# First stage of a token tower: denominators moved to ScalarE, VectorE's instructions in another order

## The chip, the cores and the metric

The kernel runs on one core of a Trainium2 chip. The metric is the device time of one execution in microseconds (us); smaller is better. The core's engines run side by side, each through its own list of instructions in order, and wait for one another by semaphores: TensorE (PE: products and transposes into PSUM banks), VectorE (DVE), ScalarE (ACT), GpSimd (POOL) and SyncE (SP, which issues transfers).

## The reference, cut to what matters

64 x 128 tokens go through an embedding, a layer with linear attention, and a layer with 16 experts. The change lies in the attention:

```python
pq, pk = (_phi(q), _phi(k))                      # phi(x) = elu(x) + 1
kv = jnp.einsum('bshd,bshm->bhmd', pk, v)
z = 1.0 / (jnp.einsum('bshd,bhd->bsh', pq, pk.sum(axis=1)) + 1e-06)
attn = jnp.einsum('bshd,bhmd,bsh->bshm', pq, kv, z)
...
h = tok(x)                                       # embedding of the tokens, 256 wide
h = h + attn(layernorm(h))                       # 16 heads of 16
h = h + ffn(layernorm(h))                        # gates, two of 16 experts, causal attention
```

`z` is one divided by the sum for each head plus 1e-6: the sums plus that constant are the denominators.

## The kernel before, in words

One tile is one sequence: 128 tokens on 128 partitions, 256 values each; there are 64 tiles (B). The kernel has three stages one after another: the first (embedding, attention, second norm, gate scores, places of the tokens with their experts; to about 360 us), the products of the experts' weights with the sorted tokens (to about 560 us), and the causal attention with the output products. The first stage also splits the experts' weights into a high part (ScalarE, L548) and a low part (VectorE, L553, `weight_lo`), one weight a step in 48 of the steps.

In the first stage every engine runs a function `step1(i)` for i from -7 on, written out, one call after another; nothing but the order of the calls and the semaphores orders the work. In one step the engines work on different tiles: the first norm of tile i+4, the attention's exponentials of tile i+3, its sums of tile i+2, the second norm of tile i+1, the gate scores of tile i. By the names used below:

- `centers` (VectorE, L1235) turns the roots that GpSimd formed (L768) into the shifts of both norms. It is the first thing of VectorE's step.
- x1 (ScalarE, L927) is the first norm of tile i+4; it waits for `centers`. TensorE turns it (L1662), ScalarE casts the turned tile (x1_T, L943, written to `split_hi`), VectorE forms the rest (x1_lo, L1310, written to `split_lo`).
- Behind x1_lo TensorE forms the q/k product (L1677 with the bias, then L1681) and the v product. In the next step ScalarE applies Relu (L917) and Exp (L921) to q and k, and VectorE adds them to phi (L1302).
- phi is turned, and key times value is summed (L1757); VectorE masks it by heads: the big kvm product (L1321) and the small one (L1323). In the next step TensorE forms the sums of numerators and denominators from both (L1709).
- VectorE then forms `den` (L1240: the sums plus 1e-6), the reciprocal (L1243, `zden`), `attn` (L1245) and the residual h2 (L1254), which SyncE stores.
- bn_stats and the aggregate of h2 (L1258, L1260), with the first norm's aggregate (L1314) and statistics (L1079), lead by `roots_in` (L1266, L1267) to GpSimd's roots and so to the `centers` of the next step.
- Every fourth tile closes a group of four for the gates. Its pieces are spread over four steps near the end of VectorE's step: `experts_chosen`, `experts_numbered`, `rows_counted` (L1205 writes `before_rows`), `rows_placed`. TensorE's part, the rank product (L1691, L1692), waits for `before_rows` and stands at the beginning of TensorE's step, ahead of the sums (L1709).

ScalarE's step is, in order: Relu, Exp, x1, x2 (the second norm, L888), the copy of v (L935), x1_T, two more copies (L948, L894), the cast of a weight (L548). VectorE's is: `centers`, `weight_lo`, phi, `den`, reciprocal, `attn`, x1_lo, first aggregate, h2, big kvm, small kvm, bn_stats of h2, its aggregate, `roots_in`, the gates' piece, statistics of the next rows. The tail of the stage (last tiles) runs interleaved with the beginning of the second stage.

Of the kernel before, what the change touches and what calls it, by code (L numbers as in the profile page):

```python
# [44 lines left out]
P = 128  # L45
# [56 lines left out]
def build(nc, x_turned, embed, W_qkv, b_qkv, W_proj, b_proj, sim_matrix, gates, q_proj, k_proj, v_proj, o_proj, out):  # L102
# [37 lines left out]
    with ExitStack() as ctx:  # L140
# [19 lines left out]
        causal_r = sb("causal_r", [P, P], F32R)  # L160
        zeros = sb("zeros", [P, C])
        minus_half = sb("minus_half", [P, E])
        eps = sb("eps", [P, 3])
        expert_no = sb("expert_no", [P, E])
        region_start = sb("region_start", [P, E])
        tile_no = sb("tile_no", [P, 1])
# [184 lines left out]
        o_scaled = sem("o_scaled")  # L351
        o_pooled = sem("o_pooled")
        o_added = sem("o_added")
        N_CONSTS = 16

        EARLY_GROUP = EARLY_TOKENS // QUAD - 1
        N_EARLY_OPS, N_EARLY_TAB = 17, 9
# [337 lines left out]
        def _(pool):  # L695
# [26 lines left out]
            pool.memset(used[:, E:E + 1], 0.0).then_inc(consts_ready, 1)  # L722
            pool.memset(eps[:, 0:2], LN_EPS).then_inc(consts_ready, 1)
            pool.memset(eps[:, 2:3], NORM_EPS).then_inc(consts_ready, 1)
            pool.memset(before_rows[:, :, :].bitcast(F32), 0.0).then_inc(consts_ready, 1)
            pool.iota(expert_no[:, :], pattern=[[1, E]], base=0, channel_multiplier=0,
                      allow_small_or_imprecise_dtypes=True).then_inc(consts_ready, 1)
# [143 lines left out]
        def _(act):  # L871
# [24 lines left out]
            def split_and_copy(i):  # L896
# [6 lines left out]
                if i.inside(PAIR_TILES) and i.p:  # L903
# [5 lines left out]
                    pair, m = y_slot(i)  # L909
                    act.copy(pair[:, m, :], ps_y[i.c % len(ps_y)][:, 0:Y]).then_inc(done["pair_copied"], 1)  # L910

            def step1(i):
                tile = i.shift(3)
                if tile.inside(B):

                    after(act, "qk_product", tile)
                    act.activation(qk_neg[:, :], ps_qk[:, :], ACT.Relu, scale=-1.0  # L917
                                   ).then_inc(done["qk_negative"], 1)
                    after(act, "qk_negative", tile)
                    after(act, "phi", tile.shift(-1))  # L920
                    act.activation(qk_e[:, :], qk_neg[:, :], ACT.Exp, scale=-1.0).then_inc(done["qk_exp"], 1)  # L921
                tile = i.shift(4)
                if tile.inside(B):
                    t = tile.c
                    after(act, "x1_turned", tile.shift(-1))
                    after(act, "centers", tile)
                    act.activation(x1[:, :], h[t % 8], ACT.Identity, scale=roots[:, t, 0:1],  # L927
                                   bias=centers[:, t, 0:1]).then_inc(done["x1_normed"], 1)
                if i.shift(1).inside(B):
                    second_norm(i.shift(1))  # L930
                tile = i.shift(3)
                if tile.inside(B):
                    after(act, "v_product", tile)
                    after(act, "kv_product", tile.shift(-1))
                    act.copy(vx[:, :, 0:P], ps_v[:, 0:C].rearrange("p (g n) -> p g n", g=G)  # L935
                             ).then_inc(done["v_copied"], 1)
                if i.c == TAIL_STEP - 1:
                    split_and_copy(Tile(-2))
                tile = i.shift(4)
                if tile.inside(B):  # L940
                    after(act, "x1_turned", tile)
                    after(act, "v_product", tile.shift(-1))
                    act.copy(x1T_s[0], ps_x1[:, 0:C]).then_inc(done["x1_T"], 1)  # L943
                tile = i.shift(3)
                if tile.inside(B):
                    after(act, "phi_q_turned", tile)
                    after(act, "attn_sums", tile.shift(-1))
                    act.copy(pqT[:, :, :].rearrange("p g t -> p (g t)"), ps_pq[:, 0:C]  # L948
                             ).then_inc(done["phi_q_T"], 1)
                if i.shift(1).inside(B):  # L950
                    second_turned(i.shift(1))
                for n in weights_at(i.c):
                    weight_hi(act, n)
# [3 lines left out]

            def tail(k):

                if k == 5:  # L960
                    second_norm(Tile(B - 2))
                if k == 8:
# [88 lines left out]
        def _(dve):  # L1051
# [183 lines left out]
                dve.scalar_tensor_tensor(centers[:, row, :], moments[:, row, :, 0], -1.0, roots[:, row, 0:2],  # L1235
                                         ALU.mult, ALU.mult).then_inc(done["centers"], 1)

            def attention_formed(tile):
                after(dve, "attn_sums", tile)
                dve.tensor_scalar(den[:, :, :], ps_sums[:, :, P:NUMW], DEN_EPS, None, ALU.add  # L1240
                                  ).then_inc(done["attn_den"], 1)
                after(dve, "attn_den", tile)
                dve.reciprocal(zden[:, :, :], den[:, :, :]).then_inc(done["attn_z"], 1)  # L1243
                after(dve, "attn_z", tile)
                dve.tensor_tensor(attn[:, :].rearrange("p (g h d) -> p g h d", g=G, d=D),  # L1245
                                  ps_sums[:, :, 0:P].rearrange("p g (h d) -> p g h d", d=D),
# [9 lines left out]
            def second_stats(tile):  # L1256
                after(dve, "h2", tile)
                dve.bn_stats(stats[:, 2 * tile.p + 1, :], h2[tile.p][:, :]).then_inc(done["ln2_stats"], 1)  # L1258
                after(dve, "ln2_stats", tile)
                dve.bn_aggr(moments[:, tile.c + 3, 1, :], stats[:, 2 * tile.p + 1, :]  # L1260
                            ).then_inc(done["ln2_moments"], 1)
# [22 lines left out]
            def step1(i):  # L1284
# [8 lines left out]
                    gates_formed()  # L1293
                if i.c == 0:
                    gate_columns_scaled()
                for n in weights_at(i.c - 1):
                    weight_lo(dve, n)
                if phi_tile.inside(B):

                    after(dve, "kv_product", phi_tile.shift(-1))  # L1300
# [1 line left out]
                    dve.scalar_tensor_tensor(phi[:, :], ps_qk[:, :], 0.0, qk_e[:, :], ALU.max, ALU.add  # L1302
                                             ).then_inc(done["phi"], 1)
                if attn_tile.inside(B):
                    attention_formed(attn_tile)
                if i.c == TAIL_STEP - 1:
                    split_and_copy(Tile(-2))
                if x1_tile.inside(B):
                    after(dve, "x1_T", x1_tile)
                    dve.tensor_tensor(x1T_s[1], ps_x1[:, 0:C], x1T_s[0].bitcast(F32), ALU.subtract  # L1310
                                      ).then_inc(done["x1_lo"], 1)
                if ln1_tile.inside(B):
                    after(dve, "ln1_stats", ln1_tile)
                    dve.bn_aggr(moments[:, ln1_tile.c, 0, :], stats[:, 2 * i.p, :]).then_inc(done["ln1_moments"], 1)  # L1314
                if attn_tile.inside(B):
                    residual_added(attn_tile)
                if phi_tile.inside(B):

                    after(dve, "attn_sums", phi_tile.shift(-1))
                    after(dve, "kv_product", phi_tile)  # L1320
                    dve.tensor_tensor(kvm[:, :, 0:P], ps_kv[:, :, 0:P],  # L1321
                                      head_mask[:, :].unsqueeze(1).broadcast_to([P, G, P]), ALU.mult)
                    dve.tensor_tensor(kvm[:, :, P:NUMW], ps_kv[:, :, P:P + 1].broadcast_to([P, G, HG]),  # L1323
                                      head_of_row[:, :].unsqueeze(1).broadcast_to([P, G, HG]), ALU.mult
                                      ).then_inc(done["kv_masked"], 1)
# [1 line left out]
                    split_and_copy(Tile(-1))  # L1327
                if attn_tile.inside(B):
                    second_stats(attn_tile)
                row = i.c + 5  # L1330
                if 0 <= row < N_ROOTS:
                    root_inputs(row, attn_tile)
# [71 lines left out]
            def tail(k):  # L1404
# [3 lines left out]
                if k == 2:  # L1408
                    experts_numbered(last_group - 2)
                if k == 3:  # L1410
                    attention_formed(Tile(B - 1))
                    residual_added(Tile(B - 1))
                    second_stats(Tile(B - 1))
                    root_inputs(N_ROOTS - 1, Tile(B - 1))
                if k == 4:
                    centers_formed(N_ROOTS - 2)
# [524 lines left out]
```

## Time and profile before

| | |
|---|---|
| time, median of 3 runs | 995.45 us (992.7 to 995.6) |
| profiled execution: time, span | 992.72 us, 990.9 us |
| TensorE busy over the span | 925.8 us (93%) |
| VectorE busy | 838.2 us (85%) |
| ScalarE busy | 600.0 us (61%) |
| GpSimd busy | 668.9 us (68%) |
| mean granted clock of TensorE | 0.987 of full speed |

The span is the profiled time from the first instruction to the last. Busy shares are means over stages of different kinds, so they are read by stretch. Consecutive instructions of VectorE and ScalarE may overlap a little in the trace: the next can start before the one in front has ended.

### The profile page before, as it was taken

How to read it: one execution, taken by the hardware profiler on the slowest of the kernel's cores; microseconds unless marked ns; L12 is line 12 of the kernel's file. 1: busy time of each engine (PE TensorE's matmuls, PEld its weight loads, DVE VectorE, ACT ScalarE, POOL GpSimd, SP SyncE). 2: the span in 40 equal slices, each digit the busy share in tenths (PEclk: the TensorE clock that was granted, in tenths of full speed). 3: DMA queues.
4: the chain of work that ended last, by engine and by line, in shares of the span. 5: the costliest groups of instructions: out<-in, count | busy, mean ns of one | idle time of the engine just before them, and what ended most of it. 6: DMA issues, size and time to landing. Idle time of an engine off the chain costs nothing.

```text
span 990.9 us, 20545 instructions
## 1 busy us (share of the span) xinstructions
PE 925.8 (93%) x5231; PEld 798.1 (81%) x5231; DVE 838.2 (85%) x2910; ACT 600.0 (61%) x1633; POOL 668.9 (68%) x881
## 2 busy tenths in 40 slices
PE   4999999999899989989999599999999999999998
PEld 4777788887777889979899578888888888888876
DVE  3789999999999987556665369999999999999998
ACT  4566676676667554435444266666666766666664
POOL 5447777777777655795000268888888888888885
PEclk9999999999999999989999889999999999999999
DMA  2113444444343349878898423333333333333231
GB/s 66 49 60 123 127 130 155 144 149 130 113 128 115 99 159 333 281 251 274 279 294 266 156 84 104 107 107 107 107 98 103 100 100 107 107 107 103 90 102 38
DMA packets 104762, 137.54 MB, mean 139 GB/s; under 512 B 13762, under 2 KB 91586, under 8 KB 104644
## 3 DMA queue, kind: packets, MB, share of 16 engines
q1 hardware_dynamic: 86196, 82.93, 26.6%
q0 software_dynamic: 18176, 52.45, 17.4%
q8 instruction: 49, 0.80, 0.3%
q10 hardware_dynamic: 272, 0.79, 0.2%
q14 instruction: 69, 0.57, 0.2%
HBM read 70.06 MB, written 66.06 MB: 137 GB/s over the span
## 4 chain that ended last, share of the span: by engine, by line
PE 60%; DVE 26%; issue 6%; POOL 3%; DMA 2%; ACT 2%; SPq 1%; POOLq 0%; DVEq 0%; ACTq 0%
PE bank L1655 16%; PE bank L1656 16%; PE bank L1657 16%; PE bank L1662 6%; DVE phi L1302 4%; DVE attn L1245 2%; DVE kvm L1321 2%; DVE stats L1258 2%; PE bank L1681 2%; DVE stats L1079 2%; DVE zden L1243 1%; PE bank L1899 1%; PE bank L1905 1%; POOL sorted_x L786 1%; DVE moments L1260 1%
## 5 line engine op out<-in xcount | busy, mean ns | idle before, releaser
L1655 PE MATMUL bank<-wo_hi,split_lo 128*128 128x512 f32 x512 | 214.6, 419 | 1.5 <-DVE split_lo L1623 0.8
L1656 PE MATMUL bank<-wo_lo,split_hi 128*128 128x512 f32 x512 | 203.3, 397 | 0.0
L1657 PE MATMUL bank<-wo_hi,split_hi 128*128 128x512 f32 x512 | 203.3, 397 | 0.0
L860 POOL DMA_INDIRECT row_y<-sorted_y,pair_now x128 | 130.7, 1021 | 31.2 <-issue 22.3
L1009 ACT ACTIVATE h<-bank,rwo 128x256 f32<-128x256 f32 x256 | 106.8, 471 | 26.5 <-PE bank L1657 13.9
L1657 PEld LDWEIGHTS bank<-wo_hi,split_hi 128*128 128x128 f32 x512 | 96.8, 189 | 23.1
L1655 PEld LDWEIGHTS bank<-wo_hi,split_lo 128*128 128x128 f32 x512 | 96.9, 189 | 21.5 <-DVE x L1592 1.6
L1592 DVE SCALAR_TENSOR_TENSOR x<-bank,rwo,x 128x256 f32<-128x256 f32 x256 | 111.1, 475 | 1.2 <-PE bank L1657 1.2
L1656 PEld LDWEIGHTS bank<-wo_lo,split_hi 128*128 128x128 f32 x512 | 97.5, 190 | 17.5
L1592 DVE SCALAR_TENSOR_TENSOR qk_e<-bank,rwo,qk_e 128x256 f32<-128x256 f32 x256 | 110.9, 474 | 0.2 <-PE bank L1657 0.2
L1655 PE MATMUL bank<-wq_hi,split_lo 128*128 x288 | 110.6, 384 | 0.0
L768 POOL TENSOR_TENSOR roots<-roots_in,minus_half 128x3 f32<-128x3 f32 x67 | 59.9, 894 | 74.4 <-DVE roots_in L1267 74.4
L917 ACT ACTIVATE qk_neg<-bank 128x512 f32<-128x512 f32 x64 | 38.3, 598 | 113.2 <-PE bank L1681 113.2
L778 POOL DMA_INDIRECT sorted_x<-row_y,position_u x80 | 80.9, 1011 | 31.1 <-issue 23.1
L1275 DVE TENSOR_TENSOR split_lo<-bank,split_hi 128x256 fp32r<-128x256 f32 x144 | 60.6, 421 | 46.1 <-ACT split_hi L901 45.0
L1656 PE MATMUL bank<-wq_lo,split_hi 128*128 x288 | 98.1, 341 | 0.0
L1657 PE MATMUL bank<-wq_hi,split_hi 128*128 x288 | 97.8, 340 | 0.0
L1009 ACT ACTIVATE phi<-bank,rwo 128x256 f32<-128x256 f32 x128 | 53.7, 471 | 68.9 <-PE bank L1657 68.9
L1681 PE MATMUL bank<-wo_hi,split_lo 128*128 128x512 f32 (+1 forms) x256 | 87.4, 342 | 0.0
L1681 PE MATMUL bank<-wo_lo,split_hi 128*128 128x512 f32 (+1 forms) x256 | 87.2, 340 | 0.0
L1681 PE MATMUL bank<-wo_hi,split_hi 128*128 128x512 f32 (+1 forms) x256 | 87.1, 340 | 0.0
L901 ACT CAST split_hi<-bank 128x256 fp32r<-128x256 f32 x144 | 53.8, 375 | 46.7 <-PE bank L1662 45.1
(242 smaller groups left out, 2529.4 us busy)
## 6 DMA issues: line engine op xcount, KB each, us to landing
sorted_y<-w_attn SPq DMA_DIRECT2D x40, 384.0 KB, 3.4
sorted_y<-row_y SPq DMA_DIRECT2D x24, 384.0 KB, 3.6
h_rows<-h SPq DMA_DIRECT2D x64, 128.0 KB, 1.7
row_x<-h_rows SPq DMA_DIRECT2D x64, 128.0 KB, 3.5
out_h<-row_x SPq DMA_DIRECT2D x64, 128.0 KB, 2.1
h<-sorted_x SPq DMA_DIRECT2D x48, 128.0 KB, 3.3
phi<-sorted_x SPq DMA_DIRECT2D x24, 128.0 KB, 3.5
qk_neg<-sorted_x SPq DMA_DIRECT2D x24, 128.0 KB
```

The costliest lines, as they stand in the source:

```text
L768: pool.tensor_tensor(roots[:, row, :], roots_in[:, row, :], minus_half[:, 0:3], ALU.pow).then_inc(done["roots"], 1)
L778: pool.indirect_dma_start(out=sorted_x, out_offset=offsets(position_u[:, t, n:n + 1]), in_=x2[t % N_X2], in_offset=None).then_inc(scattere ...
L860: pool.indirect_dma_start(out=row_y[:, 2 * tile.p + n, :], out_offset=None, in_=sorted_y, in_offset=offsets(pair_now[tile.q][:, n:n + 1])) ...
L901: act.copy(split[tile.q][0][:, :, :].rearrange("p c t -> p (c t)"), ps_turn[tile.p][:, 0:C]).then_inc(done["pair_hi"], 1)
L1009: act.mul(part[:, j, :], ps[:, j * C:(j + 1) * C], rwo[tile.p][:, e:e + 1]).then_inc(o_scaled, 1)
L1275: dve.tensor_tensor(lo, ps_turn[tile.p][:, 0:C], hi.bitcast(F32), ALU.subtract).then_inc(done["pair_lo"], 1)
L1592: dve.scalar_tensor_tensor(acc[j][:, :], src, weight, base[:, :], ALU.mult, ALU.add).then_inc(o_added, 1)
L1655: pe.matmul(ps, left[1][c], right[0][c], start=(c == 0), stop=False)
L1656: pe.matmul(ps, left[0][c], right[1][c], start=False, stop=False)
L1657: last = pe.matmul(ps, left[0][c], right[0][c], start=False, stop=(c == n - 1))
L1662: last = pe.transpose(ps[:, n * P:(n + 1) * P], piece, ident[:, :])
L1681: last = pe.matmul(ps[:, 0:hi - lo], turned[x][c], w_attn_s[w][:, c, lo:hi], start=False, stop=end)
```

## The change

The denominators move from VectorE to ScalarE: an Identity activation with the constant 1e-6 as a bias per row, between Exp and x1, waiting for the sums. A fourth column of `eps` holds the constant, so GpSimd sets one more constant. On VectorE `attention_formed` is split into the reciprocals and the rest, `second_stats` into statistics and moments, and the order of the step changes: `weight_lo` goes from behind `centers` to between the statistics and the moments of h2; `attn` goes behind x1_lo; h2 goes between the two kvm products. In the tail the last tile's denominators stand on ScalarE at the same place (k = 3).

```diff
@@ constants
-        eps = sb("eps", [P, 3])
+        eps = sb("eps", [P, 4])
-        N_CONSTS = 16
+        N_CONSTS = 17
+            pool.memset(eps[:, 3:4], DEN_EPS).then_inc(consts_ready, 1)
@@ ScalarE
+            def denominators(tile):
+                after(act, "attn_sums", tile)
+                after(act, "attn_z", tile.shift(-1))
+                act.activation(den[:, :, :], ps_sums[:, :, P:NUMW], ACT.Identity, bias=eps[:, 3:4]
+                               ).then_inc(done["attn_den"], 1)
...
                     act.activation(qk_e[:, :], qk_neg[:, :], ACT.Exp, scale=-1.0).then_inc(done["qk_exp"], 1)
+                if i.shift(2).inside(B):
+                    denominators(i.shift(2))
...
+                if k == 3:
+                    denominators(Tile(B - 1))
@@ VectorE
-            def attention_formed(tile):
-                after(dve, "attn_sums", tile)
-                dve.tensor_scalar(den[:, :, :], ps_sums[:, :, P:NUMW], DEN_EPS, None, ALU.add
-                                  ).then_inc(done["attn_den"], 1)
+            def attention_inverses(tile):
                 after(dve, "attn_den", tile)
                 dve.reciprocal(zden[:, :, :], den[:, :, :]).then_inc(done["attn_z"], 1)
+
+            def attention_formed(tile):
                 after(dve, "attn_z", tile)
...
-                for n in weights_at(i.c - 1):
-                    weight_lo(dve, n)
...
                 if attn_tile.inside(B):
-                    attention_formed(attn_tile)
+                    attention_inverses(attn_tile)
...
                     dve.tensor_tensor(x1T_s[1], ps_x1[:, 0:C], x1T_s[0].bitcast(F32), ALU.subtract
                                       ).then_inc(done["x1_lo"], 1)
+                if attn_tile.inside(B):
+                    attention_formed(attn_tile)
                 if ln1_tile.inside(B):
...
-                if attn_tile.inside(B):
-                    residual_added(attn_tile)
                 if phi_tile.inside(B):
...
                     dve.tensor_tensor(kvm[:, :, 0:P], ps_kv[:, :, 0:P],
                                       head_mask[:, :].unsqueeze(1).broadcast_to([P, G, P]), ALU.mult)
+                if attn_tile.inside(B):
+                    residual_added(attn_tile)
+                if phi_tile.inside(B):
                     dve.tensor_tensor(kvm[:, :, P:NUMW], ps_kv[:, :, P:P + 1].broadcast_to([P, G, HG]),
...
                 if attn_tile.inside(B):
                     second_stats(attn_tile)
+                for n in weights_at(i.c - 1):
+                    weight_lo(dve, n)
+                if attn_tile.inside(B):
+                    second_moments(attn_tile)
...
                 if k == 3:
+                    attention_inverses(Tile(B - 1))
                     attention_formed(Tile(B - 1))
                     residual_added(Tile(B - 1))
                     second_stats(Tile(B - 1))
+                    second_moments(Tile(B - 1))
```

## Rows read from the trace of the kernel before

**Rows 1.** Stretches: length, busy us (instructions) by engine, granted clock, DMA share, GB/s.
```profile
core 0: us, PE busy (x) PEld busy (x) DVE busy (x) ACT busy (x) POOL busy (x), PEclk, DMA share, GB/s
0.00:20.00 20.00, 7.97 (x28) 6.37 (x29) 7.44 (x22) 8.03 (x16) 12.76 (x37) 1.00 0.24 75
60.00:350.00 290.00, 266.98 (x1749) 231.03 (x1748) 271.04 (x1275) 194.59 (x479) 205.27 (x209) 1.00 0.40 125
420.00:430.00 10.00, 5.28 (x23) 4.87 (x22) 2.60 (x6) 1.90 (x5) 9.33 (x17) 0.76 0.63 198
```
**Rows 2.** Instructions in order of time (start, length in us), ScalarE, 48 steps apart.
```profile
71.16 0.58 ACT L927 ACTIVATE x<-h,centers,roots 128x256 f32<-128x256 f32 x1
...
329.45 0.63 ACT L921 ACTIVATE qk_e<-qk_neg 128x512 f32<-128x512 f32 x1
329.99 0.58 ACT L927 ACTIVATE x<-h,centers,roots 128x256 f32<-128x256 f32 x1
```
**Rows 3.** In order of time, one step of ScalarE: Relu, Exp, x1, x1_T, next Relu.
```profile
187.91 0.60 ACT L917 ACTIVATE qk_neg<-bank 128x512 f32<-128x512 f32 x1 [1.65 <-PE bank L1681]
188.54 0.63 ACT L921 ACTIVATE qk_e<-qk_neg 128x512 f32<-128x512 f32 x1
189.13 0.60 ACT L927 ACTIVATE x<-h,centers,roots 128x256 f32<-128x256 f32 x1
...
190.38 0.37 ACT L943 CAST split_hi<-bank 128x256 fp32r<-128x256 f32 x1
...
193.25 0.60 ACT L917 ACTIVATE qk_neg<-bank 128x512 f32<-128x512 f32 x1 [1.65 <-PE bank L1681]
```
**Rows 4.** In order of time, the same step of VectorE, to the next centers.
```profile
188.89 0.14 DVE L1235 SCALAR_TENSOR_TENSOR centers<-moments,roots 128x2 f32<-128x2 f32 x1
188.95 0.41 DVE L553 TENSOR_TENSOR wq_lo<-raw,wq_hi 128x256 fp32r<-128x256 f32 x1
189.28 0.68 DVE L1302 SCALAR_TENSOR_TENSOR phi<-bank,qk_e 128x512 f32<-128x512 f32 x1
189.89 0.16 DVE L1240 TENSOR_SCALAR den<-bank 128x16 f32<-128x16 f32 x1
190.08 0.25 DVE L1243 RECIPROCAL zden<-den 128x16 f32<-128x16 f32 x1
190.37 0.42 DVE L1245 TENSOR_TENSOR attn<-bank,zden 128x256 f32<-128x256 f32 x1
190.78 0.42 DVE L1310 TENSOR_TENSOR split_lo<-bank,split_hi 128x256 fp32r<-128x256 f32 x1
191.12 0.17 DVE L1314 BATCH_NORM_AGGREGATE moments<-stats 128x2 f32<-128x6 f32 x1
...
191.93 0.42 DVE L1258 BATCH_NORM_STATS2 stats<-h 128x6 f32<-128x256 f32 x1
192.38 0.18 DVE L1260 BATCH_NORM_AGGREGATE moments<-stats 128x2 f32<-128x6 f32 x1
192.67 0.17 DVE L1266 TENSOR_SCALAR roots_in<-moments 128x2 f32<-128x2 f32 x1
...
193.15 0.80 DVE L1205 TENSOR_TENSOR before_rows<-before_rows,top_two 128x16 fp32r<-128x16 f32 x4
...
194.20 0.14 DVE L1235 SCALAR_TENSOR_TENSOR centers<-moments,roots 128x2 f32<-128x2 f32 x1
```
**Rows 5.** In order of time, TensorE: sums, q/k product, rank product, the next sums.
```profile
188.53 0.63 PE L1709 MATMUL bank<-kvm,pqT 128*128 128x136 f32 x4
...
191.35 0.47 PE L1677 MATMUL bank<-bias,ones_r 128*128 128x512 f32 x1
...
194.00 0.30 PE L1691 MATMUL bank<-top_two,earlier_r 128*128 128x64 f32 x1
...
194.24 0.71 PE L1709 MATMUL bank<-kvm,pqT 128*128 128x136 f32 x4
```
**Rows 6.** By line, ScalarE's 16-column operations: duration ns min/median/max, first and last start.
```profile
L874 ACT ACTIVATE gate_bias<-gate_tmp x1: 216/216/216, 5.6 to 5.6; 128x16 f32<-128x16 f32 x1
...
L1042 ACT ACTIVATE rwo<-routing,psumm x64: 307/310/323, 574.6 to 978.8; 128x16 f32<-128x16 f32 x64
```

More of the change, by code:

```diff
@@ L1258, in second_stats, with second_moments @@
                 dve.bn_stats(stats[:, 2 * tile.p + 1, :], h2[tile.p][:, :]).then_inc(done["ln2_stats"], 1)
+            def second_moments(tile):
                 after(dve, "ln2_stats", tile)
```

## The prediction, made before the result was known

> **What bounds the kernel now.** I read the stretches first: from 60 to 350 us, the body of the first stage, TensorE is busy for 267.0 of 290 us and VectorE for 271.0, both over 92% [rows 1]. Shares that close do not say which engine sets the step, so I followed one step of each engine in order of time. The step repeats: from the x1 of one step (71.16) to the x1 48 steps on (329.99) is 258.83 us, 5.39 us a step [rows 2].
>
> Two closed loops run through a step. I count from start to start.
>
> *The ScalarE loop.* x1 (189.13) is followed by its turn on TensorE and by the cast of the turned tile, x1_T (190.38): 1.25. VectorE's x1_lo begins 0.40 later (190.78), which is the cast's 0.37 and 0.03 more: x1_lo starts when the cast lets it, and not before [rows 3, 4]. Behind x1_lo TensorE starts the q/k product (191.35), and ScalarE's Relu of it starts at 193.25, 2.47 after x1_lo; the Exp 0.63 after the Relu; the next x1, where nothing else holds it, 0.54 after the Exp (329.45 to 329.99) [rows 2 to 5]. Sum: 1.25 + 0.40 + 2.47 + 0.63 + 0.54 = 5.29.
>
> *The VectorE loop.* x1 also needs `centers`, which VectorE forms first in its step: centers at 188.89, x1 at 189.13, 0.24 [rows 3, 4]. So from centers to x1_lo there are 0.24 + 1.25 + 0.40 = 1.89 us that VectorE's order can't shorten. From x1_lo round to the next centers (190.78 to 194.20) are 3.42. Sum: 5.31.
>
> The kernel sits where both loops are nearly equal. What VectorE does inside the 1.89 us is free as long as it fits: weight_lo, phi, den, reciprocal and attn stand there now (188.95 to 190.78) and just fill it [rows 4]. What it does after x1_lo is paid in full.
>
> **The change part by part.**
>
> *Order of VectorE.* The new order is centers, phi, reciprocal, x1_lo, attn, first aggregate, the big kvm product, h2, the small kvm product, bn_stats of h2, weight_lo, its aggregate, and the rest as before. Two instructions move from the free side of x1_lo to the paid side: attn (190.37, 0.42 long) and weight_lo (188.95, 0.41). Neighbours that don't read each other start 0.08 before the end of the one in front (weight_lo takes 0.33 from start to start, x1_lo's successor starts 0.34 after it), so they add 0.34 + 0.34. Given back: bn_stats to its aggregate takes 0.45 now, since the aggregate reads it (0.42 + 0.03); with weight_lo between them bn_stats takes 0.34, so -0.11. Lost again: bn_stats of h2 now comes two behind h2 and starts when h2 is written, about +0.03, the size of the wait in front of the reciprocal (189.89 + 0.16 to 190.08). In all 0.34 + 0.34 - 0.11 + 0.03 = +0.60 from x1_lo to centers [rows 4]. The ends: 0.68 if nothing is given back; 0.41 if the pause behind that aggregate (192.38, 0.18 long, the next at 192.67, 0.19 more than in a close pair) goes as well.
>
> The 0.11 between a dependent and an independent pair is this trace's [rows 4]. The Trainium skill, page "VectorE: DVE Perf Modes", section "The DRAIN you can't avoid", says that a wait between chained operations costs nothing beyond the flush that every operation pays; the trace disagrees by that 0.11. By the page the addition would be 0.34 + 0.34 = 0.68, and the 48 steps with a weight would lose 3.8 us more.
>
> The denominator's 0.16 and its wait in front of the reciprocal, and the wait from reciprocal to attn, lie in the 1.89 and give nothing back: VectorE is ready for x1_lo some 0.06 + 0.61 + 0.28 = 0.95 us after centers and then stands still for about 0.9 us, until the cast comes. Without that cover they would be worth 0.19 + 0.11.
>
> New VectorE loop: 3.42 + 0.60 + 1.89 = 5.91 for this step; over the 36 of the 48 steps that have no rank product I take +0.59 (0.01 of a step was slack of centers).
>
> *Denominators on ScalarE.* The instruction stands between Exp and x1, so x1, x2, the v copy and the casts queue behind its wait for the sums. The sums end at 189.16 (188.53 + 0.63), 1.25 after the Relu and just at the end of the Exp (189.17) [rows 3, 5]. The trace of before has no such operation; the nearest are ScalarE's 16-column operations, 0.216 without a scale per row and 0.310 with one [rows 6]. Less 0.10 of overlap with x1 (the Exp is 0.63 long, x1 starts 0.54 behind it) they delay x1 by 0.12 to 0.21. I take 0.15, nearer the first, and 0.05 for the semaphore (0.03 to 0.10). An operation that is hidden whole would be 0.
>
> The Trainium skill, page "ScalarE: Activation LUTs", section "What ACT_TABLE_LOAD costs", prices an ACTIVATE with a bias per row at 280 ns + 0.833 ns a column, with 93 ns overlapped: an estimate of 0.20 for 16 columns, which would add 0.05 to the steps that this loop bounds, 1.2 us in all.
>
> ScalarE loop in a plain step: 2.47 + 1.25 + 0.05 + 0.15 + 1.25 + 0.40 = 5.57. That is under VectorE's 5.9 while weights are split, so there the ScalarE part costs nothing by itself. In the 11 steps up to 76 us no weight is split; there VectorE's addition is only 0.26 (no weight_lo) and ScalarE's loop decides: 5.57 against about 5.28, ten times +0.29, and +1.0 once where a rank product falls: 3.9 us. The last three steps: about 0.7.
>
> *Where both meet: the rank steps.* In every fourth step TensorE makes a rank product ahead of the sums. It waits for VectorE's `before_rows` (193.15 + 0.80 = 193.95; rank at 194.00), and the sums end at 194.95, 4.17 behind x1_lo [rows 4, 5]. Nothing was late by that: VectorE came to the sums only behind phi. Now ScalarE waits for them in front of x1, and before_rows itself comes 0.60 later. So x1_lo to sums 4.77, semaphore 0.05, denominators 0.15, then 1.65 to x1_lo: 6.62 instead of 5.31, +1.31. There are 12 such steps in the 48: 15.7 us.
>
> *The rest.* h2 comes about 0.7 us later behind x1_lo, and with it SyncE's store of h2 and, behind that in its queue, the next weight's load; the weight's cast is the last thing of ScalarE's step, so I cost this at nothing; a weight that came late would add its lateness to weight_lo. The one memset more in the set-up and the denominators in the tail I also take as nothing (under 0.5 us together).
>
> *Sum.* 36 x 0.59 = 21.2; rank steps 15.7; steps without weights 3.9; last steps 0.7: 41.5 us. Later stages start later and keep their length. The profiled execution took 992.72 us (span 990.9); 992.72 + 41.5 = 1034.2. That is 2.7 below the median of the runs shown, 995.45, and at their lowest, 992.7; the median of the new runs may lie either way, and I put the forecast at 1035.
>
> **The rivals.**
> 1. *VectorE is relieved, as its 93% suggests.* Without den and the dependent pairs VectorE has 0.4 us less to issue. If the order did not hold x1_lo to the cast, the step would sink to the ScalarE loop of 5.29, at most 0.10 x 48 = 5 us: 990. Against it: x1_lo starts 0.03 behind the cast already, so an earlier place can't make it earlier [rows 3, 4]. The Trainium skill, page "Perfetto Trace Analysis", section "Optimizing Scalar/DVE Operations", advises moving work to ScalarE when VectorE is saturated; by that rule this rival wins. Chance 0.04.
> 2. *Only ScalarE's loop pays.* If the instructions behind x1_lo found room, because centers stopped deciding x1, then plain steps cost 5.57 - 5.39 = 0.18 (6.5 us), rank steps 2.47 + 1.70 + 0.05 + 0.15 + 1.65 = 6.02, +0.71 (8.5 us), others 4: 19 us, 1012. Against it: in the step shown centers alone explains x1. Chance 0.12.
> 3. *It cancels out*, within 0.3%: both additions lie in waits that I read wrongly. Chance 0.04.
> 4. *The clock falls.* TensorE's share in the stage sinks from 92% to about 81% (times 5.39 / 6.15). In the ten microseconds from 420 TensorE was idle for 4.7 and the granted clock was 0.76; over the first 20 us, 40% busy, it was 1.00 [rows 1]. If a tenth of the clock went, some 3.5 us of TensorE work in each of 60 steps would cost 21 us more: 1055. Chance 0.06.
>
> **How the numbers follow.** The forecast has 0.74. Its own range: with an addition of 0.41 in place of 0.60 the 48 steps lose 0.19 x 48 = 9.1 us less, 1025; with 0.68 they lose 3.8 more, and the upper prices on ScalarE (0.06 + 0.05 in 24 steps) 2.6 more, 1041. To hold 8 in 10 the range reaches down to rival 2: 1011 to 1042. Chances: slower by over 0.3% (about what a measurement of this kernel tells from no change) 0.74 + 0.12 + 0.06 = 0.92, the same 0.04, faster 0.04.
>
> **What would show it.** Right: in the new trace x1_lo still starts 0.03 behind the cast, but with some 0.9 us of VectorE idle before it, released by ScalarE (over 40 us in the stage); x1_lo to centers near 4.0; steps of 5.9 to 6.1, rank steps near 6.6; VectorE's share in the stage near 80%; denominators on ScalarE of 0.2 to 0.3 us that start right behind the sums; the loss complete by the end of the first stage. Wrong: x1_lo without idle time before it (rival 1), rank steps like the others (rival 2), a granted clock under 1.00 (rival 4), or later stages that give time back.

## The result, and the profile after

The changed kernel takes 1037.43 us (median of 4 runs, 1036.1 to 1038.38); the kernel before, run beside it, 995.32. The ratio is 1.0428, 95% interval 1.0407 to 1.0449: slower by 4.3%. The profiled execution took 1038.38 us with a span of 1036.5, against 992.72 and 990.9 before, so the two traces differ by 45.6 us of span. The medians leave out two far slower runs, one of weight_only (1801.41) and one of the kernel before (1275.7).

The stretch from 60 to 350 us, in the columns of [rows 1], and the longest waits between 60 and 335 us (engine, line, what it waited for: us in all, times, longest us) for VectorE and ScalarE:

```profile
60.00:350.00 290.00, 239.43 (x1531) 207.42 (x1530) 223.93 (x1070) 184.50 (x468) 177.74 (x184) 0.98 0.36 112
...
DVE split_lo L1320 <- ACT split_hi L952: 46.1, 44, 1.3
DVE zden L1251 <- ACT den L916: 3.9, 11, 0.6
...
ACT den L916 <- PE bank L1728: 12.3, 12, 1.3
ACT x L936 <- DVE centers L1246: 6.9, 20, 0.6
```

VectorE has fallen from 271.0 busy us [rows 1] to 223.9, TensorE from 267.0 to 239.4: no engine is short of room, and yet the step is longer. `split_lo` is x1_lo. It now has VectorE idle in front of it in 44 steps, 46.1 us in all between 60 and 335 us, and ScalarE's cast ends that wait. ScalarE in turn stands 12 times in front of `den`, which waits for TensorE's sums.

One rank step and the plain step behind it, all engines in order of time (the columns of [rows 2]). They answer to [rows 3 to 5]:

```profile
186.95 0.42 DVE L1320 TENSOR_TENSOR split_lo<-bank,split_hi 128x256 fp32r<-128x256 f32 x1 [0.98 <-ACT split_hi L952]
187.29 0.41 DVE L1255 TENSOR_TENSOR attn<-bank,zden 128x256 f32<-128x256 f32 x1
...
188.47 0.43 DVE L1268 BATCH_NORM_STATS2 stats<-h 128x6 f32<-128x256 f32 x1
188.81 0.41 DVE L553 TENSOR_TENSOR wq_lo<-raw,wq_hi 128x256 fp32r<-128x256 f32 x1
189.13 0.17 DVE L1272 BATCH_NORM_AGGREGATE moments<-stats 128x2 f32<-128x6 f32 x1
...
189.89 0.80 DVE L1216 TENSOR_TENSOR before_rows<-before_rows,top_two 128x16 fp32r<-128x16 f32 x4
190.05 0.63 ACT L928 ACTIVATE qk_e<-qk_neg 128x512 f32<-128x512 f32 x1
190.75 0.30 PE L1710 MATMUL bank<-top_two,earlier_r 128*128 128x64 f32 x1 [0.54 <-DVE before_rows L1216]
190.95 0.14 DVE L1246 SCALAR_TENSOR_TENSOR centers<-moments,roots 128x2 f32<-128x2 f32 x1
190.99 0.71 PE L1728 MATMUL bank<-kvm,pqT 128*128 128x136 f32 x4
191.74 0.27 ACT L916 ACTIVATE den<-bank,eps 128x16 f32<-128x16 f32 x1 [1.06 <-PE bank L1728]
191.91 0.59 ACT L936 ACTIVATE x<-row_x,centers,roots 128x256 f32<-128x256 f32 x1
193.15 0.38 ACT L952 CAST split_hi<-bank 128x256 fp32r<-128x256 f32 x1
193.56 0.42 DVE L1320 TENSOR_TENSOR split_lo<-bank,split_hi 128x256 fp32r<-128x256 f32 x1 [1.26 <-ACT split_hi L952]
...
196.66 0.63 ACT L928 ACTIVATE qk_e<-qk_neg 128x512 f32<-128x512 f32 x1
197.32 0.27 ACT L916 ACTIVATE den<-bank,eps 128x16 f32<-128x16 f32 x1
197.48 0.14 DVE L1246 SCALAR_TENSOR_TENSOR centers<-moments,roots 128x2 f32<-128x2 f32 x1
197.72 0.60 ACT L936 ACTIVATE x<-row_x,centers,roots 128x256 f32<-128x256 f32 x1
198.97 0.37 ACT L952 CAST split_hi<-bank 128x256 fp32r<-128x256 f32 x1
199.37 0.42 DVE L1320 TENSOR_TENSOR split_lo<-bank,split_hi 128x256 fp32r<-128x256 f32 x1 [0.99 <-ACT split_hi L952]
```

*The rank step* runs from x1_lo at 186.95 to x1_lo at 193.56, 6.61 us. Follow what ended last: before_rows ends at 190.69, the rank product starts at 190.75, the sums behind it end at 191.70; the denominators start at 191.74, x1 at 191.91, and the cast lets x1_lo go 1.65 after x1. centers had been there since 191.09: it no longer decides.

*The plain step* runs from 193.56 to 199.37, 5.81 us. Here the denominators start at 197.32 and would let x1 go 0.17 later, at 197.49; it waits for centers and starts at 197.72, 0.24 after centers' start. centers itself comes 3.92 after x1_lo, since attn (187.29 in the step above) and weight_lo (188.81) now stand between them.

Step lengths from x1_lo to x1_lo over the whole stage, means in us, with their count; the very first step (6.87 before, 6.62 after) is left out:

| | first 11, no weight | 36 plain | 12 rank | last 3 | last x1_lo of the stage |
|---|---|---|---|---|---|
| before | 5.35 | 5.40 | 5.38 | 5.75 | 354.38 |
| after | 5.71 | 6.04 | 6.66 | 6.09 | 397.76 |
| all of it | +4.0 | +23.3 | +15.3 | +1.0 | +43.4 |

The stage ends 43.4 us later, of 45.6 in the span. The last 2 us come before the third stage: from the last x1_lo to the first of ScalarE's `rwo` operations ([rows 6], L1042) it is 220.3 us before and 222.7 after, and from there to the end of the span 416 in both.

### The profile page after: what moved, and what is told of

Same layout as the page of the kernel before. It is cut to its first block, busy times and chain, and to the rows that moved or that the text cites. A ratio compares the mean times of both kernels' runs of the same rounds, so it can differ in the third digit from the quotient of the medians.

```text
span 1036.5 us, 20609 instructions
## 1 busy us (share of the span) xinstructions
PE 930.8 (90%) x5231; PEld 802.6 (77%) x5231; DVE 817.4 (79%) x2846; ACT 618.7 (60%) x1697; POOL 663.7 (64%) x882
## 4 chain that ended last, share of the span: by engine, by line
PE 55%; DVE 19%; issue 8%; ACT 7%; POOL 7%; DMA 3%; SPq 1%; ACTq 0%; POOLq 0%; DVEq 0%
PE bank L1674 14%; PE bank L1675 14%; PE bank L1676 14%; PE bank L1681 5%; PE bank L1700 3%; DVE split_lo L1320 2%; DVE h L1264 2%; ACT split_hi L952 2%; DVE stats L1268 2%; ACT row_y L889 2%; POOL row_y L861 2%; DVE wq_lo L553 1%; POOL sorted_x L787 1%; PE bank L1728 1%; ACT x L889 1%
## 5 line engine op out<-in xcount | busy, mean ns | idle before, releaser
L861 POOL DMA_INDIRECT row_y<-sorted_y,pair_now x128 | 133.3, 1042 | 31.2 <-issue 22.3
L779 POOL DMA_INDIRECT sorted_x<-row_y,position_u x80 | 78.7, 983 | 31.6 <-issue 23.1
L1681 PE MATMUL bank<-ident,x 128*128 128x128 f32 x200 | 41.3, 289 | 54.9 <-ACT x L936 54.9
```

What stands on the lines that cost most here:

```text
L779: pool.indirect_dma_start(out=sorted_x, out_offset=offsets(position_u[:, t, n:n + 1]), in_=x2[t % N_X2], in_offset=None).then_inc(scattere ...
L861: pool.indirect_dma_start(out=row_y[:, 2 * tile.p + n, :], out_offset=None, in_=sorted_y, in_offset=offsets(pair_now[tile.q][:, n:n + 1])) ...
L1681: last = pe.transpose(ps[:, n * P:(n + 1) * P], piece, ident[:, :])
```

## The experiments

The theory is that of the prediction: two loops. In VectorE's, a step is the way from x1_lo to centers plus 1.89 us. In ScalarE's, when it carries the denominators, a step is x1_lo to Relu (2.47), Relu to the end of the sums, 0.04 and 0.17 to x1, 1.65 to x1_lo. The longer one is the step. The rival is that only one of the two is real: that the loss comes whole from ScalarE's new wait, or whole from VectorE's order. A further question was whether the two loops are what held the kernel before, or only what holds the one after. den_only, order_only, weight_only and attn_back ran beside the kernel before at 993.9 us, the kernels below them in the table beside it at 993.29; the changed kernel has its own comparison above.

All kernels, with the two measured quantities from which the loops are computed:

| | us | ratio (95%) | plain: x1_lo to centers | plain step | rank: Relu to end of sums | rank step |
|---|---|---|---|---|---|---|
| before | 993.9, 993.29 | | 3.50 | 5.40 | 1.77 | 5.38 |
| after | 1037.43 | 1.0428 (1.0407 to 1.0449) | 4.11 | 6.04 | 2.33 | 6.66 |
| den_only | 1011.82 | 1.0172 (1.0148 to 1.0196) | 3.50 | 5.59 | 1.74 | 6.07 |
| order_only | 1026.26 | 1.0319 (1.0300 to 1.0338) | 4.07 | 5.97 | 2.34 | 5.96 |
| weight_only | 1002.92 | 1.0078 (1.0052 to 1.0103) | 3.70 | 5.59 | 1.97 | 5.58 |
| attn_back | 1027.41 | 1.0332 (1.0314 to 1.0349) | 3.95 | 5.84 | 2.17 | 6.50 |
| attn_and_h2_back | 1016.31 | 1.0233 (1.0211 to 1.0255) | 3.72 | 5.66 | 1.95 | 6.28 |
| high_first | 991.45 | 0.9979 (0.9969 to 0.9989) | 3.50 | 5.39 | 2.11 | 5.39 |
| spread_pairs | 989.0 | 0.9959 (0.9944 to 0.9974) | 3.35 | 5.32 | 1.63 | 5.31 |
| both_loops | 981.52 | 0.9878 (0.9857 to 0.9899) | 3.35 | 5.24 | 1.96 | 5.24 |

The plain means of the changed kernel hold three steps in which TensorE's clock fell, those of order_only and attn_back one each (last section).

### Denominators alone (den_only)

The kernel before, with the denominators on ScalarE behind Exp and VectorE's order kept.

```diff
+            def denominators(tile):
+                after(act, "attn_sums", tile)
+                after(act, "attn_z", tile.shift(-1))
+                act.activation(den[:, :, :], ps_sums[:, :, P:NUMW], ACT.Identity, bias=eps[:, 3:4]
...
+                if i.shift(2).inside(B):
+                    denominators(i.shift(2))
...
-                dve.tensor_scalar(den[:, :, :], ps_sums[:, :, P:NUMW], DEN_EPS, None, ALU.add
-                                  ).then_inc(done["attn_den"], 1)
```

> The kernel before with the denominators on ScalarE and VectorE's order untouched but for the removed instruction. Theory of two loops: VectorE's paid side does not change, ScalarE's loop becomes 2.47 + 1.25 + 0.04 + 0.17 + 1.65 = 5.58 in plain steps (5.40 before) and 2.47 + 1.70 + 0.04 + 0.17 + 1.65 = 6.03 in rank steps (5.38 before), 5.58 in most early ones: +7 and +8 and +4 us, some 1014 us. Rival, that the new order alone loses and ScalarE has room for the denominators (it is busy 61%): 995 within 0.3%. Rival, that VectorE's work sets the stage: 0.19 less in 62 steps, 984.

It measured 1011.82, 17.9 us above the kernel before. The plain step is ScalarE's loop: 2.47 + 1.25 + 0.04 + 0.17 + 1.65 = 5.58 (measured 5.59); the rank step 2.47 + 1.74 + 0.04 + 0.17 + 1.65 = 6.07 (measured 6.07). A rank step on ScalarE, in order of time:

```profile
135.53 0.63 ACT L928 ACTIVATE qk_e<-qk_neg 128x512 f32<-128x512 f32 x1
136.65 0.28 ACT L916 ACTIVATE den<-bank,eps 128x16 f32<-128x16 f32 x1 [0.49 <-PE bank L1717]
136.82 0.59 ACT L936 ACTIVATE x<-row_x,centers,roots 128x256 f32<-128x256 f32 x1
```

The operation itself is the small part, 0.17 from its start to x1's. The larger one is that x1 now cannot start before the sums end: 0.49 us of waiting in this step, where x1 used to follow Exp by 0.54.

### The order alone (order_only)

The changed kernel with the denominators put back on VectorE, ahead of the reciprocals; all of the new order stays.

```diff
-            def denominators(tile):
-                after(act, "attn_sums", tile)
...
             def attention_inverses(tile):
+                after(dve, "attn_sums", tile)
+                dve.tensor_scalar(den[:, :, :], ps_sums[:, :, P:NUMW], DEN_EPS, None, ALU.add
+                                  ).then_inc(done["attn_den"], 1)
                 after(dve, "attn_den", tile)
```

> The new order of VectorE with the denominators left on VectorE, directly ahead of the reciprocal. Theory of two loops: from x1_lo to centers 0.60 more, so plain steps 5.99 instead of 5.40, rank steps no longer coupled through ScalarE and near 5.97 instead of 6.66; early steps nearly as before: +21 +7 +2 us, some 1026 us, and about 0.9 us of VectorE standing still in front of x1_lo less the denominator's 0.19. Rival, that ScalarE's instruction is the loss: 995 or a little under, since dependent pairs are spread.

It measured 1026.26. Both rank and plain steps are 5.96 to 5.97, VectorE's loop: 4.07 + 1.89 = 5.96. In the rank steps the sums end as late as in the changed kernel, 2.34 against 2.33 after the Relu, and it does not matter. One of them, in order of time, and the wait of x1 between 60 and 335 us:

```profile
137.71 0.63 ACT L921 ACTIVATE qk_e<-qk_neg 128x512 f32<-128x512 f32 x1
138.40 0.30 PE L1702 MATMUL bank<-top_two,earlier_r 128*128 128x64 f32 x1 [0.54 <-DVE before_rows L1205]
138.65 0.71 PE L1720 MATMUL bank<-kvm,pqT 128*128 128x136 f32 x4
138.84 0.60 ACT L927 ACTIVATE x<-row_x,centers,roots 128x256 f32<-128x256 f32 x1 [0.50 <-DVE centers L1235]
...
ACT x L927 <- DVE centers L1235: 24.7, 45, 0.9
```

x1 starts at 138.84, half a microsecond before these sums end (139.36); it waits for centers, 45 times, 24.7 us. So the late sums cost a rank step 0.70 (6.66 against 5.96) only through the denominators in ScalarE's queue. In the plain steps the denominators add nothing on top of the order: without the steps of lower clock the means are 5.97 and 5.96.

The parts do not add up: 17.9 us for the denominators alone and 32.4 for the order alone would be 50.3, and the change costs 42.1 in its own comparison. In plain steps the longer loop hides the other one: +0.19 for the denominators alone, +0.56 for the order alone, +0.57 for both (without the steps of lower clock).

### One of the two moved instructions (weight_only)

The kernel before, with weight_lo moved from behind centers to between the statistics and the moments of h2.

```diff
-                for n in weights_at(i.c - 1):
-                    weight_lo(dve, n)
...
                 if attn_tile.inside(B):
                     second_stats(attn_tile)
+                for n in weights_at(i.c - 1):
+                    weight_lo(dve, n)
+                if attn_tile.inside(B):
+                    second_moments(attn_tile)
```

> The kernel before with weight_lo alone moved to between the statistics and the moments of h2. Theory of two loops: paid side + 0.34 - 0.11 = + 0.23 in the 48 steps with a weight, a third of a microsecond of VectorE standing still in front of x1_lo: +11 us, 1006 us. Rival, that taking the wait out between the statistics and the moments helps: 0.11 less in 48 steps, 990.

It measured 1002.92. x1_lo to centers grew by 0.20 (3.50 to 3.70), and the 48 plain and rank steps by 0.19 and 0.20, 9.2 us, against 9.0 between the medians (5 to 10 by the interval of the ratio). An instruction of 0.41 us, moved from the covered side of x1_lo to the other, costs half of its length here: the part that it takes from the wait between the statistics and their aggregate comes back.

### attn put back (attn_back), and h2 with it (attn_and_h2_back)

The changed kernel with attn back in front of x1_lo:

```diff
                 if attn_tile.inside(B):
                     attention_inverses(attn_tile)
+                    attention_formed(attn_tile)
...
-                if attn_tile.inside(B):
-                    attention_formed(attn_tile)
```

> The changed kernel with attn put back ahead of x1_lo; everything else of the change stays. Theory of two loops: of the 0.60 on VectorE's paid side 0.34 go, so plain steps are set by both loops near 5.67, rank steps near 6.33 (the rows counted come 0.34 earlier): 25 us over the kernel before, 1020 us. Rival, that the place of attn does not matter: 1037.

A miss: 1027.41, 7 us above what was expected. x1_lo to centers is 3.95. With attn gone from behind x1_lo, the big kvm product stands directly behind the first aggregate and is ready before its input. In order of time:

```profile
334.46 0.63 PE L1775 MATMUL bank<-vx,phi 128*128 128x130 f32 x4
334.63 0.42 DVE L1321 TENSOR_TENSOR split_lo<-bank,split_hi 128x256 fp32r<-128x256 f32 x1 [0.80 <-ACT split_hi L952]
334.97 0.17 DVE L1325 BATCH_NORM_AGGREGATE moments<-stats 128x2 f32<-128x6 f32 x1
335.20 0.42 DVE L1330 TENSOR_TENSOR kvm<-bank,head_mask 128x256 f32<-128x256 f32 x1
```

The aggregate ends at 335.14 and a next operation that does not depend on it would start at 335.06, as the one behind x1_lo does 0.08 before its end; kvm starts at 335.20, 0.11 behind the end of TensorE's kv product (335.09). If that is the cause, h2 in front of kvm, where the kernel before has it, should cover the wait. The second kernel puts it back as well:

```diff
+                if attn_tile.inside(B):
+                    residual_added(attn_tile)
                 if phi_tile.inside(B):
...
-                if attn_tile.inside(B):
-                    residual_added(attn_tile)
-                if phi_tile.inside(B):
```

> The run attn_back with h2 put back ahead of the big kvm product as well. In attn_back that product stood 0.43 behind x1_lo and waited some 0.14 for TensorE's key-value product. Theory: that wait is what was missing from the 0.34, so plain steps 5.68 and rank steps 6.35, 7 us under attn_back: 1020 us. Rival, that attn's 0.34 is only half paid whatever stands behind it: 1027 as before.

It measured 1016.31, 4 us under what was expected, and x1_lo to centers is 3.72, that of weight_only (3.70), as it should be when weight_lo is the only thing left. The same place, in order of time:

```profile
337.19 0.63 PE L1774 MATMUL bank<-vx,phi 128*128 128x130 f32 x4
337.36 0.42 DVE L1321 TENSOR_TENSOR split_lo<-bank,split_hi 128x256 fp32r<-128x256 f32 x1 [0.53 <-ACT split_hi L952]
337.70 0.17 DVE L1325 BATCH_NORM_AGGREGATE moments<-stats 128x2 f32<-128x6 f32 x1
337.79 0.39 DVE L1264 TENSOR_TENSOR h<-row_x,attn 128x256 f32<-128x256 f32 x1
338.10 0.42 DVE L1332 TENSOR_TENSOR kvm<-bank,head_mask 128x256 f32<-128x256 f32 x1
```

h2 runs from 337.79 while the kv product ends (337.82), and kvm follows at its usual distance. h2's place cost 0.23 us a step in attn_back, more than the expectation put on it. The wait in the lines shown is 0.14 of it; another 0.07 lies in the distances between h2, the two kvm products and the statistics, which differ in the two orders. In the changed kernel attn stood in the gap instead of h2, so there the same wait was covered: in its step above the kv product ends at 187.42, and kvm starts at 187.71, 0.09 behind the aggregate's start.

The rank steps of both kernels fit ScalarE's loop with the sums' own lateness: 4.33 + 2.17 = 6.50 and 4.33 + 1.95 = 6.28, as measured (4.33 is 2.47 + 0.04 + 0.17 + 1.65).

### Shortening each loop of the kernel before (high_first, spread_pairs, both_loops)

If the kernel before sits where two loops are nearly equal, then shortening one should give little, and both more than the sum. high_first shortens ScalarE's: TensorE runs the products that don't read x1_lo before it waits for x1_lo.

```diff
+                after(pe, "x1_T", tile)
...
-                    for x, w, end in ((1, 0, False), (0, 1, False), (0, 0, c == CH - 1)):
-                        last = pe.matmul(ps[:, 0:hi - lo], turned[x][c], w_attn_s[w][:, c, lo:hi], start=False,
-                                         stop=end)
+                    for w in (1, 0):
+                        pe.matmul(ps[:, 0:hi - lo], turned[0][c], w_attn_s[w][:, c, lo:hi], start=False, stop=False)
+                after(pe, "x1_lo", tile)
+                for c in range(CH):
+                    last = pe.matmul(ps[:, 0:hi - lo], turned[1][c], w_attn_s[0][:, c, lo:hi], start=False,
+                                     stop=(c == CH - 1))
```

> The kernel before with only TensorE's order changed: bias and high products of q, k and v go ahead of the wait for x1_lo, the low products last. Theory of two loops: x1_lo leaves ScalarE's loop, which becomes shorter by TensorE's pause of 0.2 in front of the product (5.08), but VectorE's loop stays and sets nearly every step: 1 to 2 us less, not to be told from no change. Rival, that TensorE (92% busy) sets the stage: 0.2 in 60 steps, 12 us less.

spread_pairs shortens VectorE's: the first aggregate goes between the denominators and the reciprocals, in front of x1_lo, and the small kvm product between the statistics and the moments of h2.

```diff
                     denominators(attn_tile)
+                if ln1_tile.inside(B):
+                    after(dve, "ln1_stats", ln1_tile)
+                    dve.bn_aggr(moments[:, ln1_tile.c, 0, :], stats[:, 2 * i.p, :]).then_inc(done["ln1_moments"], 1)
...
                     second_stats(attn_tile)
+                if phi_tile.inside(B):
+                    dve.tensor_tensor(kvm[:, :, P:NUMW], ps_kv[:, :, P:P + 1].broadcast_to([P, G, HG]),
...
+                if attn_tile.inside(B):
+                    second_moments(attn_tile)
```

> The kernel before with two small instructions of VectorE moved into its dependent pairs and nothing carried from one side of x1_lo to the other in the wrong direction: the first aggregate goes between den and reciprocal, the small kvm product between the statistics and the moments of h2. Denominators stay on VectorE. Theory of two loops: paid side 0.09 + 0.08 = 0.17 shorter, but plain steps sink only to ScalarE's loop of 5.28: 5 us less, 989. Rival, VectorE alone: 0.17 + in 60 steps, 10 us less.

both_loops has both edits.

> high_first and spread_pairs together. Theory of two loops: ScalarE's loop 5.08, VectorE's 0.17 shorter: 11 us less, 983; more than the sum of the two alone (about 6.5). Rival, effects add: 6 to 7 us less.

Measured: 991.45 (-1.8 us), 989.0 (-4.3), and together 981.52 (-11.8), nearly twice the sum of 6.1. Each fits. In high_first the way from x1_lo to Relu falls from 2.47 to 2.14, and what x1 waits for changes; its waits between 60 and 335 us:

```profile
ACT qk_neg L917 <- PE bank L1685: 68.0, 51, 1.6
ACT x L927 <- DVE centers L1235: 17.0, 51, 0.7
```

x1 waits for centers in 51 steps, 17.0 us, and the plain step stays at VectorE's 3.50 + 1.89 = 5.39. Only the first 11 steps, where no weight is split, become shorter (5.35 to 5.22). The rival's 12 us, TensorE setting the stage, are not there. In spread_pairs VectorE's loop falls to 3.35 + 1.89 = 5.24, but the step to 5.32 only: ScalarE's loop, 5.29 in the prediction, now holds it, and x1 starts within 0.03 of 0.54 behind the Exp in 34 of the 48 steps (25 in the kernel before). In both_loops the step is 5.24, VectorE's loop to the hundredth. The stretch from 60 to 350 us of both_loops:

```profile
60.00:350.00 290.00, 262.35 (x1802) 234.48 (x1801) 274.17 (x1314) 201.96 (x489) 211.25 (x215) 1.00 0.41 129
```

VectorE's 274.2 busy us are only 3.1 more than before [rows 1], with 1314 instructions in the stretch against 1275.

The 0.15 us that spread_pairs takes out of VectorE's way (3.50 to 3.35) has two parts. The first aggregate now stands ahead of x1_lo, between the denominators and the reciprocals, and the small kvm product between the statistics and the moments of h2. In order of time:

```profile
337.66 0.16 DVE L1240 TENSOR_SCALAR den<-bank 128x16 f32<-128x16 f32 x1
337.74 0.17 DVE L1312 BATCH_NORM_AGGREGATE moments<-stats 128x2 f32<-128x6 f32 x1
337.86 0.25 DVE L1245 RECIPROCAL zden<-den 128x16 f32<-128x16 f32 x1
...
339.50 0.42 DVE L1260 BATCH_NORM_STATS2 stats<-h 128x6 f32<-128x256 f32 x1
339.83 0.16 DVE L1334 TENSOR_TENSOR kvm<-bank,head_of_row 128x16 f32<-128x16 f32 x1
339.95 0.18 DVE L1264 BATCH_NORM_AGGREGATE moments<-stats 128x2 f32<-128x6 f32 x1
```

The aggregate starts 0.08 before the denominators end. The reciprocals start 0.20 after the start of the denominators, where they started 0.19 after it with nothing in between [rows 4]: an instruction of 0.17 us goes into the chain for 0.01. From the statistics to their aggregate it takes 0.45 with the small product in between, as it did without it [rows 4]. Two things are mixed here, though: the small product is gained by the pair alone, while the aggregate also goes from the paid side of x1_lo to the covered one. No run separates them.

The Trainium skill, page "VectorE: DVE Perf Modes", section "The DRAIN you can't avoid", reports of eight copies that a semaphore after each "costs nothing extra here"; the same section says that "A next op that is not held starts earlier". In this trace an instruction that waits for the one just ahead starts 0.03 behind its end, and one that does not read it 0.08 before its end [rows 4]: 0.11 a pair, and in the two pairs above other work filled that time. The prediction's 0.68 by the page rests on the first of the two sentences alone; the 0.57 measured is below it.

So the idea that results should not be read by the next operation is sound; what counts is what is put in between, and on which side of x1_lo it stood before.

## Why the prediction was right

The forecast was 1035, and 1037.43 was measured, within its range and on the side that it held 0.92 likely. Its parts, one by one:

- *Which loops.* Shown: 5.24 in both_loops, 5.39 in high_first and 5.32 in spread_pairs are what the two loops make of the edits. Shares of busy time alone, both engines over 92% [rows 1], would not have said so.
- *Order of VectorE, +0.60 from x1_lo to centers.* Measured 0.61 in the mean of the plain steps, but that holds three steps with a lower clock. Without them it is 0.57 against the same 33 steps before, and the steps are 5.97 against 5.40, +0.57 where +0.59 was put. The weight alone measured 0.20 for a predicted 0.34 - 0.11 = 0.23. The cost in the plain steps, 36 x 0.59 = 21.2, came out at 23.3: 33 x 0.57 = 18.8, and 4.5 from the three steps, at 6.80 (1.5 each).
- *The 0.11 given back by the separated pair.* Without it the addition would have been 0.68 or more; it is 0.57, and weight_only (0.20 for an instruction that takes 0.34) and spread_pairs show it coming back.
- *Denominators.* 0.15 from start to start was taken between 0.12 and 0.21; it is 0.17 (0.274 us long, median of 64). The semaphore, 0.05, is 0.04. The sum, 0.20, is 0.21. The Trainium skill's figure ("ScalarE: Activation LUTs", "What ACT_TABLE_LOAD costs"), by which 0.20 was estimated for the first of these, is 0.03 above the trace.
- *Rank steps, 6.62.* Nine of the twelve are 6.61 or 6.62; in the step shown the sums end 4.75 after x1_lo, where 4.77 was put. Three others are 6.72 to 6.90, so that the mean is 6.66. From 5.38 this is 15.3 us, predicted 15.7. That the coupling goes through ScalarE's queue is shown by order_only.
- *Steps without weights, 3.9, and the last, 0.7.* 4.0 and 1.0.
- *What was put at nothing.* The 2 us between the last x1_lo and the third stage were not predicted. In the runs here the span's change differs from that of the last x1_lo by -0.3 (attn_and_h2_back) to +3.8 us (den_only), and the runs of the kernel before spread over 2.9 (992.7 to 995.6). The cause stays open.

The rivals: *Only ScalarE's loop pays* gave 1012, and that is what den_only measures (1011.82); as an account of the whole change it falls with order_only and weight_only. *VectorE is relieved* falls: VectorE is relieved, but only into 46.1 us of idle time before x1_lo. *It cancels out* falls with the time itself. *The clock falls* was costed as all or nothing, with 3.5 us of TensorE work a step that no row shows; in truth it happened at three places for some microseconds each. The sign named for it, a granted clock under 1.00, did appear (0.98 from 60 to 350 us), and it is a term that should have been in the sum.

So the mechanism was right, and the closeness of the total is in part luck. At the same place in the other groups of four the step is 5.82 in the median, so of the 4.5 us of the three steps about 3 are the clock's (an estimate: three times 6.80 - 5.82). Without these the stage would have grown by some 40.5 us, 1 under the sum's 41.5; the clock's 3 us and the 2 us before the third stage, for neither of which the sum has a term, make up the span's 45.6. Between the medians it is 42.1, since the profiled run of the kernel before was its fastest and that of the changed kernel its slowest.

## What to carry to other kernels

Before moving work to a less busy engine, or away from a dependent neighbour, close the loops: follow one step from an event to the same event of the next step on each engine, and write down what stands on the covered side and what on the paid side of each wait. An operation put between two others of an in-order queue brings its own wait with it, and its input may be late only in every fourth step. Where two loops are nearly equal, an edit of one seems worthless until the other is shortened too: -1.8 and -4.3 us alone, -11.8 together.

## What the runs showed of the hardware beside this

TensorE's granted clock fell in the changed kernel's first stage, where it had been 1.00 before. Around 168 us, in stretches of 2 us (the columns of [rows 1]), and one product of the same shape before and in it:

```profile
166.00:168.00 2.00, 1.41 (x13) 1.27 (x13) 0.47 (x2) 1.73 (x6) 1.39 (x3) 0.96 0.24 66
168.00:170.00 2.00, 2.00 (x8) 1.81 (x8) 1.67 (x7) 0.91 (x4) 0.94 (x1) 0.50 0.39 135
...
162.36 0.39 PE L1700 MATMUL bank<-wo_hi,split_lo 128*128 128x512 f32 x1
...
169.29 0.63 PE L1700 MATMUL bank<-wo_hi,split_lo 128*128 128x512 f32 x1
```

The clock is 0.50 from 168 to 170 us, which is its lower level, 1.2 GHz, and the 512-column product takes 0.63 us from start to end in place of 0.39. Before this TensorE had been idle for 0.85 us waiting for x1 (until 160.57), 0.54 for before_rows (until 165.28) and 0.59 for x1 (until 167.17). It happened in three plain steps, each directly behind a rank step; x1_lo to Relu is 3.69 in them, where it is 2.47 elsewhere. Pauses of the same length stand in rank steps where the clock stayed, as in the one shown above (0.54 until 190.75), so the length of the pauses alone does not explain which steps fall. In order_only and attn_back the clock fell once each between 60 and 350 us, from 320.43 and from 309.17: in attn_back again in a plain step behind a rank step, in order_only in one that is not, with TensorE idle before it for 1.02 us (until 312.45) and 1.23 (until 318.65), both times waiting for x1. So it needs neither the denominators on ScalarE nor a rank step just in front. What decides it is open. In the kernel before and in the other six no such fall shows between 60 and 350 us.
